# Rows of shifts moved from `nmt` into `qt` by four transfers from SBUF to SBUF, in place of a store to DRAM and a load back

## The reference, cut to what matters

```
Q1, Q2, K1, K2: 8 features each per head;  scaling = 1/sqrt(8)
A1 = (Q1 @ K1.T) * scaling                # causal mask: -inf above the diagonal
A2 = (Q2 @ K2.T) * scaling
attn = softmax(A1) - lam * softmax(A2)
O = attn @ V;  O = O / rms(O) * rms_scale * 0.2
x = x + ga * (O @ W_o.T)
```

## Time and profile before

| | us |
|---|---|
| median of 3 timed runs | 1507.72 |
| lowest and highest of them | 1501.75, 1516.68 |
| profiled execution, whole | 1502.92 |
| profiled execution, span | 1501.2 |
| TensorE busy (matmuls) | 1331.8 |
| VectorE, ScalarE, GpSimd busy | 1129.3, 959.6, 874.8 |
| moved by DMA | 155.31 MB |

### The profile page before, as it was taken

How to read it: one execution, slowest core, us unless ns; L and a number is a source line. 1 busy time by engine, 2 the same in 40 slices (tenths; PEclk the granted TensorE clock), 3 DMA queues, 4 the chain that set the end, 5 groups by cost and what they waited for, 6 DMA issues and landing times. The chain is left out here.

```text
span 1501.2 us, 41440 instructions
## 1 busy us (share of the span) xinstructions
PE 1331.8 (89%) x13722; PEld 1080.7 (72%) x13849; DVE 1129.3 (75%) x2858; ACT 959.6 (64%) x2007; POOL 874.8 (58%) x1287
## 2 busy tenths in 40 slices
PE   2798999999999999999999999998469999999983
PEld 1476767767777667777677666775369999999982
DVE  4677887888888888888878888886366666666646
ACT  1276777777777777777777777777245555555540
POOL 3155576767767677676767667676524334333436
PEclk9899999999999999999999999999579999999995
DMA  3434554455544544444433444331612111111219
GB/s 102 110 87 121 128 137 126 110 136 131 154 110 124 150 119 113 94 125 116 121 101 98 121 117 124 91 89 45 114 50 56 51 53 52 51 53 52 54 27 331
DMA packets 169457, 155.31 MB, mean 103 GB/s; under 512 B 20499, under 2 KB 146713, under 8 KB 169284
## 3 DMA queue, kind: packets, MB, share of 16 engines
q1 hardware_dynamic: 148344, 124.67, 32.2%
q0 software_dynamic: 8704, 16.93, 3.8%
q10 hardware_dynamic: 12240, 11.55, 2.8%
HBM read 87.78 MB, written 66.34 MB: 103 GB/s over the span
## 5 line engine op out<-in xcount | busy, mean ns | idle before, releaser
L1013 ACT ACTIVATE probs<-p_exp 128x512 f32<-128x512 f32 x768 | 446.8, 601 | 187.2 <-PE p_exp L839 167.8
L1443 POOL TENSOR_SCALAR_AFFINE_SELECT probs<-probs 128x256 f32<-128x256 f32 (+1 forms) x768 | 365.1, 485 | 297.6 <-ACT probs L1013 289.6
L1210 DVE TENSOR_REDUCE mx<-p_max 128x2 f32<-128x512 f32 x512 | 351.4, 687 | 164.9 <-PE p_max L813 163.5
L665 POOL DMA_INDIRECT pair_out<-probs,v x144 | 142.4, 989 | 222.6 <-ACT probs L562 198.6
L811 PE MATMUL p_max<-kt,qt 96*128 96x256 bf16 x1024 | 199.3, 276 | 40.9 <-DVE mx L1210 19.8
L862 PE MATMUL p_out<-probs,v 128*32 128x256 f32 (+1 forms) x4096 | 221.1, 333 | 13.6 <-POOL probs L1443 7.5
L839 PE MATMUL p_exp<-qt,kt 100*128 100x256 bf16 x1024 | 196.9, 274 | 17.1 <-DMA qt<-max_parts 12.7
L1213 DVE TENSOR_REDUCE mx<-p_max 128x4 f32<-128x512 f32 x256 | 173.0, 676 | 1.4 <-PE p_max L822 1.3
L862 PEld LDWEIGHTS p_out<-probs,v 128*32 128x32 f32 x4096 | 112.3, 109 | 84.9 <-POOL probs L1443 23.7
L1453 POOL DMA_INDIRECT rows_sorted<-h,idx x128 | 132.5, 1035 | 37.4 <-ACT probs L1013 28.6
L811 PEld LDWEIGHTS p_max<-kt,qt 96*128 96x128 bf16 x1024 | 89.6, 101 | 81.7 <-DVE mx L1210 25.2
(11 more groups left out here) (168 smaller groups left out, 2808.5 us busy)
## 6 DMA issues: line engine op xcount, KB each, us to landing
qt<-q_parts SPq DMA_DIRECT2D x64, 384.0 KB
q_parts<-part_h SPq DMA_DIRECT2D x96, 128.0 KB, 2.0
kt<-k_parts SPq DMA_DIRECT2D x128, 96.0 KB
v<-rows_sorted SPq DMA_DIRECT2D x72, 130.0 KB
q_parts<-part_m SPq DMA_DIRECT2D x64, 128.0 KB, 2.0
kt<-k_parts SPq DMA_DIRECT2D x128, 64.0 KB
kt<-pair_out SPq DMA_DIRECT2D x16, 512.0 KB, 9.3
mods<-mod_rows SPq DMA_DIRECT2D x32, 192.0 KB
```

Of the source, the lines that this page charges most:

```text
L665: nc.gpsimd.indirect_dma_start(pair_out, bass.IndirectOffsetOnAxis(rows_in[:, j.slot, t, DIM:DIM + 1].bitcast(U32), 0), rows_out[:, j.slot ...
L1013: nc.scalar.activation(probs[:, g % 2, k, :], p_exp[:, k, :], ACT.Exp, scale=SCALE).then_inc(exp_done.sem, 1)
L1210: m = V.reduce_max(mx[:, w, 1, :, h8:h8 + 1].rearrange("p t o -> p (t o)"), p_max[:, bank, :].rearrange("p (t k) -> p t k", t=2), AX.X, ne ...
L1443: G.affine_select(out=blocks, in_=blocks, compare_op=ALU.is_ge, fill=zero, base=0, pattern=[[0, 2 if k < 2 else 4], [1, P]], channel_multi ...
```

## The change

The DRAM tensor `max_parts` goes. In `move_max`, the store, the wait and the load are replaced by four transfers straight from `nmt` to `qt`. Each takes 8 partitions of `nmt` (the 8 heads of one shift row, 512 bytes each) into one partition of `qt` (4096 bytes). The semaphore `nm_loaded` therefore counts to 64 per half and batch, and `nm_saved` goes; ScalarE's copy into `nmt` waits for `nm_loaded` of the batch before in place of `nm_saved`.

```diff
-        max_parts = dram("max_parts", [NB, 2, SHIFT_ROWS, HU, SEQ], BF16)
...
-        nm_saved = ev("nm_saved", 32)
-        nm_loaded = [ev(f"nm_loaded{w}", 16) for w in range(2)]
+        nm_loaded = [ev(f"nm_loaded{w}", 16 * SHIFT_ROWS) for w in range(2)]
...
             def move_max(b, w):
 
                 wait(sp, nmt_ready, b, w + 1)
-                sp.dma_start(max_parts[bass.ds(b.n, 1), w].rearrange("a r h k -> (a r h) k"),
-                             nmt[:, w, :]).then_inc(nm_saved.sem, 16)
-                wait(sp, nm_saved, b, 16 * (w + 1))
-                sp.dma_start(qt[QK_ROWS:ALL_ROWS, 2 * b.par + w, :, :],
-                             max_parts[bass.ds(b.n, 1), w].rearrange("a r h k -> (a r) h k")
-                             ).then_inc(nm_loaded[w].sem, 16)
+                for r in range(SHIFT_ROWS):
+                    sp.dma_start(qt[QK_ROWS + r:QK_ROWS + r + 1, 2 * b.par + w, :, :],
+                                 nmt[r * HU:(r + 1) * HU, w, :]).then_inc(nm_loaded[w].sem, 16)
...
             def copy_max(b, w):
                 wait(act, nm_ps, b, w + 1)
-                wait(act, nm_saved, b.plus(-1), 16 * (w + 1))
+                wait(act, nm_loaded[w], b.plus(-1))
```

## The result

The kernel after takes 1485.22 us (median of 4 runs, 1480.73 to 1486.25) against 1504.74 us before: a ratio of 0.9877, with a 95% interval of 0.9835 to 0.9918. That is 19.5 us less. I had forecast 7.0 us less and a range down to 1488 us; the direction was right, the size was not. The profiled execution took 1486.25 us with a span of 1484.5 us.

What follows compares the result with a forecast made beforehand. TensorE was taken to set the pace, stalling for `qt` rows in the attention stage. Gains of 3.1 + 4.8 - 0.9 = 7.0 us from 1505.3 us gave 1498.3 us, range 1488 to 1508 us, forecast chance 0.66.

Steps and rivals of the forecast that it cites:

- What bounds the kernel: Attention stage: TensorE busy 728.12 of 775.3 us; waits at line 839 for `qt` rows, 16.9 us in 17 places.
- Second leg and landing: SyncE's load back: its removal wins 1.8 us in arrival; the last row lands 0.5 us after today's store.
- Issue: SyncE's four transfers: 0.24 to 0.37 us each, 1.2 to 1.5 us together; fourth starts 0.9 to 1.1 us after first.
- Queue behind, ScalarE's copy, DRAM traffic: SyncE's later issues come 2.5 us forward, ScalarE's copy waits for previous landing, 16 KB DRAM transfers go: each gains nothing.
- What a stall is worth: 25 iterations after 190 us: 10.9 us of stalls cost 3.1 us, so removing them gains 3.1 us.
- give-back of 0.65 us per stall: After each of 12 stalls the next iteration is spared short waits, which gives back 0.65 us.
- Ahead of 190 us: First iterations: five stalls of 6.0 us give 3.2 us, plus 1.6 us for the lowered clock: 4.8 us.
- What is left: Boundaries with little slack: rows landing after today's store leave small stalls; 0.9 us subtracted from the gain.
- Everything counts: Rival: no give-back; 16.9 us of stalls and 1.6 us of clock make 18.5 us, 1487 us; chance 0.10.
- No earlier: Rival: the four land as late as the load back, 1.8 us after the store; 1505 us; chance 0.17.
- slower: Rival: last row lands 1 us later than load back, all 32 boundaries stall; +17 us, 1522 us; chance 0.07.

Runs made afterwards that it cites:

- third sitting: Kernels before and after unchanged, after with SyncE waiting in both halves, and before with first half stored early, second direct: 1505.49, 1479.21, 1483.21, 1482.47 us.
- fourth sitting: Only first half direct, only second half direct, late_issue, and the kernel after unchanged: 1501.88, 1511.91, 1516.31, 1497.88 us, beside a before of 1511.84 us.
- the fifth: direct_early and the kernel after unchanged: 1561.33 and 1495.44 us, beside a before of 1499.71 us.
- late_issue: Kernel after, with modulation rows and x issued ahead of the first half's four transfers: 1516.31 us, ratio 1.0028.
- early_store: Kernel before, with the first half's store issued ahead of the next unit's loads and its load back behind them: 1483.12 us, ratio 0.988.
- direct_early: Kernel after, with the first half's four transfers issued ahead of the first unit's loads: 1561.33 us, ratio 1.0397.

## Why the prediction was right and wrong

**What bounds the kernel: right.** TensorE sets the pace, and the rows that it waits for are the first half's, at slot 0. Direct rows in the second half alone change nothing (0.9997 and 0.9986).

**Second leg and landing: right.** I had the last row land 0.5 us behind today's store, that is 3.69 + 0.5 = 4.2 us behind the first issue; the medians are 4.2 in the trace after and 4.3 in the third sitting. I had set this against a load back at 5.5 us; in the third sitting its median is 5.5, so the rows come 1.2 us earlier from the issue on, where I had 1.3.

**Issue: too low, without harm.** 0.63 us and 0.69 with the gap, in place of 0.24 to 0.37; the fourth starts 2.06 us after the first, not 0.9 to 1.1. I had bounded a shape that the trace lacks by loads out of DRAM. The landing runs beside the issuing, so the sum survived it. The rule that I weighed, of the Trainium skill, DMA: Bandwidth & Descriptors, section Rules for kernel authors, is to merge small transfers into one large, since under 64 KB one pays mostly overhead. The traces agree with it on SyncE's time (2.69 us for four against 0.31 and 0.24), and it was no guide to the arrival, where two legs one after the other cost more than four side by side.

**Queue behind, ScalarE's copy, DRAM traffic: right at nothing.** The wait for `part_l` fell from 175.0 to 150.0 us and still covers the issues; an added store costs nothing (1485.19 us). With 2.69 us of issues in place of my 1.2 to 1.5, SyncE's later transfers come forward by 1.2 us at the boundary of 772.70 (worked out: 776.63 against 775.39), and not by 2.5. That this gains nothing was right: a wait of SyncE at that place costs nothing (1481.49 us).

**What a stall is worth: here the prediction failed.** The term that I had at 3.1 us, the gain after 190 us, measured 14.2 us in the pair of the result and 17.4 us in the pair of the third sitting. I put 10.9 us of stalls at 3.1, by comparing with five iterations in which line 839 showed no wait, and taking their 30.89 us for what an iteration of the kernel after would take. They had no stall for rows but they had late signals; the trace of the kernel after had none of these, and its iteration is 30.36. So my give-back of 0.65 us per stall was not a property of the stall. Without late signals, 17.1 us of stalls cost 17.4 us, and the kernel before has 17.8 us of stalls to lose behind 191 us, not 10.9. Of the 14.2 us, 9.0 are stalls gone (10.9 to 1.9) and the other 5.2 go with the late signals, which the trace of after lacks and the change does not remove. With late signals the term was nearer the truth: in the fourth sitting the kernel after is 0.4 us ahead in these iterations of a kernel with 9.1 us of stalls. There and in the fifth the whole gain was 14.0 and 4.3 us; in the third it was 22.5 us.

**Ahead of 190 us: too high in the pair of the result, by chance.** I expected 4.8 us. The trace after kept three early stalls and its clock fell again with them (0.66 from 124 to 128 us, 0.62 from 158.6 to 162), so 0.4 us came out; in the third sitting it was 9.2 us. The four traces of the kernel after reach the seventh marker between 181.40 and 190.09 us, the two of before at 190.47 and 190.58.

One of the three stalls of the trace after, and the busy time with the granted clock (third figure from the right) around two of them:

```profile
125.22 0.57 PE L834 MATMUL p_exp<-qt,kt 100*128 100x256 bf16 x2 [1.56 <-DMA qt<-nmt]
```
```profile
124.00:128.00 4.00, 2.78 (x15) 2.10 (x16) 1.86 (x5) 1.65 (x3) 0.41 (x1) 0.66 0.87 250
...
158.60:162.00 3.40, 3.40 (x33) 2.03 (x31) 1.92 (x3) 2.14 (x4) 1.96 (x4) 0.62 0.95 230
```

**What is left: of the right order.** 0.9 us allowed for; 1.9 us in 3 places in the trace after, 0.7 us in 2 in the third sitting.

**The rivals.** "Everything counts" came nearest, with 18.5 us; its mechanism, that a stall costs its full length, holds in the 25 iterations of the third sitting. That its sum fits the 19.5 us of the result is in part luck: in the profiled pair of the result 5.2 us go with the late signals, and the stalls ahead of 190 us, whose clock it counts in, gave 0.4 us. I had given it 0.10 on the strength of that 3.1 of 10.9. "No earlier" and "slower" did not occur; the last row of the kernel after lands 5.4 us behind the first issue at the latest (5.46 in the third sitting), just short of the 5.5 us that I had named as the point of the slower case.

**What stays open.** How much the change gives depends on the sitting: 0.9847 in one without late signals, 0.988 and 0.9953 in two with them. What brings late signals I cannot say. All kernels of each of the five sittings had them or none had, and as each sitting had its own chip, it may be the chip. In the pair of the result the trace of before, taken ahead of the prediction, has them and that of after has not. They befall matmuls that start from 0.2 us ahead to some 1.2 us behind the start of one of GpSimd's four scatters in an iteration, which stand there in the other traces too. The kernels that moved mods and x to the middle of the iteration or added a store ran in a sitting without late signals, so whether these transfers matter was not tried, nor was a kernel without scatters. Nor is it shown why a stall cost nothing beside late signals in one kernel and nearly its length in late_issue, or why early_store kept 30.37 us an iteration in a sitting with late signals (1483.12 us, where two direct kernels took 1494); it was never run beside the kernel after. A hint, not tested: among the traces with late signals, those whose first half goes through DRAM have 39 to 60 of them, those with it direct 63 to 76 (direct_early 29). So the direct way may be the dearer one wherever signals are late. No kernel tried beats the kernel after beyond doubt.

## What to carry to other kernels

Before taking "the iteration without the stall" as the floor, look at what else such an iteration waits for: here VectorE stood idle 0.43 us although its input had been started over 1 us before, and reading past it cost the forecast more than its own size. A transfer that arrives on the edge of its need stalls by the scatter of its issue; 1.5 us of earlier arrival took nearly all of it away, by either way, and 2.7 us taken from the queue at the wrong place cost 66 us. Where the increments of the semaphore are in the trace, set their times against the need at every boundary: they tell which one will stall, where totals of waits tell little. Run one kernel in two sittings, on two chips, before putting a difference of 1% between traces down to the kernel.

## What the hardware showed that I had not expected

A transfer from 8 SBUF partitions of 512 bytes into one partition of 4096 bytes keeps SyncE busy for 0.63 us (256 issues, 629 to 1337 ns), against 0.31 us for the store of 32 partitions and 0.24 us for the load of 4. Its data are in place 1.8 us after the start of the last issue at the shortest (3.83 less 2.06 us), as long as the load back from DRAM took (1.83 us). In direct_early, where SyncE has no unit load queued ahead of the four, the median from the first issue to the last row is no longer than that (3.82 us), so that over half of the way is SyncE's own issuing; with the loads ahead it is 4.33 us.

Signals of finished matmuls that otherwise come 0.29 us after the start came 0.95 to 1.8 us after it near GpSimd's scatters, in some sittings and not in others (60 in 25 iterations in the trace of before, none in that of the third sitting), with the clock granted in full (1.00). The kernel after took 10.9 and 14.1 us more for its 25 iterations in the sittings with them (770.98 and 774.18 against 760.08).
